# A tower of attention and experts on one core: waits per half and per expert, the last two pairs' expert copies on ScalarE alone, new slots for the last stage

## The reference, cut to what is computed

```python
B, S, C = 16, 512, 64            # 16 sequences of 512 tokens, 64 channels
x  = fourier_concat(ids)         # 24 features of a token
h  = LN(relu(x @ W1 + b1) @ W2 + b2) * gamma + beta + 0.1 * (x @ Wres + bres)
h  = h + attn(layernorm(h))      # 8 heads, scores 512x512, softmax, @ v, out weights Wo
f  = layernorm(h)
w  = top-2 softmax of (relu(f @ router_w1 + b) @ router_w2 + b)   # of 6 experts
y_e = relu(relu(f @ e1 + b1) @ e2 + b2) @ e3 + b3                 # every expert e
out = h + sum over the two chosen experts of w_e * y_e
```

## Time and profile before

| | us |
|---|---|
| median of 3 runs | 707.37 |
| lowest and highest | 705.65, 707.96 |
| the profiled execution, its own time | 705.38 |
| its span, first to last instruction | 703.6 |
| TensorE busy in the span | 650.5 |
| VectorE busy | 546.5 |
| ScalarE busy | 470.0 |
| GpSimd busy | 277.9 |

### The profile page before, as it was taken

One profiled execution on the slowest core, in us unless ns is written; L12 is line 12 of the kernel. 1 busy time (PEld: TensorE's weight loads), 2 busy tenths in 40 slices (PEclk: granted clock), 3 DMA queues, 4 the chain that ended last, 5 costly groups with the idle time before them and its releaser, 6 DMA issues.

```text
span 703.6 us, 26738 instructions
## 1 busy us (share of the span) xinstructions
PE 650.5 (92%) x11632; PEld 370.6 (53%) x11632; DVE 546.5 (78%) x1078; ACT 470.0 (67%) x1183; POOL 277.9 (39%) x354
## 2 busy tenths in 40 slices
PE   5789999999999999999999999999999999999974
PEld 4445555445645465545654465454664446554652
DVE  5687878787797877878787887978878788687657
ACT  2678885975668665886658766687558866678321
POOL 1242215315652175502853146620764119211173
PEclk9899999999999999999999999999999999999999
DMA  4000000000000000000000000000000000000001
GB/s 164 1 3 3 1 3 3 3 2 2 18 2 2 2 3 18 2 2 2 17 5 2 2 3 18 2 2 2 3 18 2 2 2 3 18 2 3 3 2 32
DMA packets 9428, 6.66 MB, mean 9 GB/s; under 512 B 8672, under 2 KB 8800, under 8 KB 9184
## 3 DMA queue, kind: packets, MB, share of 16 engines
q1 hardware_dynamic: 9312, 4.97, 2.4%
HBM read 2.87 MB, written 2.10 MB: 7 GB/s over the span
## 4 chain that ended last, share of the span: by engine, by line
PE 60%; DVE 22%; ACT 7%; issue 6%; POOL 4%; DMA 0%; SPq 0%; DVEq 0%; ACTq 0%; POOLq 0%
PE s_bank L525 23%; PE s_bank L494 17%; DVE nmax L899 8%; ACT p L786 5%; PE s_bank L609 5%; DVE e2t L1111 3%; PE s_bank L684 3%; PE s_bank L673 2%; PE s_bank L506 2%; DVE st L916 2%; PE s_bank L708 1%; DVE hatt L1095 1%; PE s_bank L588 1%; PE s_bank L535 1%; ACT e1t L834 1%
## 5 line engine op out<-in xcount | busy, mean ns | idle before, releaser
L786 ACT ACTIVATE p<-s_bank,nmax 128x512 f32<-128x512 f32 x512 | 347.8, 691 | 146.9 <-DVE nmax L899 145.8
L899 DVE TENSOR_REDUCE nmax<-s_bank 128x1 f32<-128x512 f32 x512 | 325.5, 681 | 50.2 <-PE s_bank L494 49.6
L494 PE MATMUL s_bank<-kf,g 64*64 64x512 f32 x2048 | 260.9, 594 | 6.4 <-DVE y L1126 2.8
L525 PE MATMUL s_bank<-p,woz 64*64 64x256 f32 x4096 | 247.1, 377 | 10.0 <-POOL woz L349 4.4
L525 PEld LDWEIGHTS s_bank<-p,woz 64*64 64x64 f32 x4096 | 163.6, 133 | 124.8 <-issue 45.9
L349 POOL TENSOR_TENSOR woz<-cst,rz 128x256 f32<-128x256 f32 x126 | 74.6, 613 | 264.0 <-DVE rz L905 264.0
L494 PEld LDWEIGHTS s_bank<-kf,g 64*64 64x64 f32 x2048 | 74.2, 133 | 91.3 <-issue 48.1
L786 ACT ACTIVATION_READ_ACCUMULATOR p<-s_bank,nmax 128x1 f32 x512 | 105.3, 206 | 0.0
L911 DVE STREAM_TRANSPOSE m<-s_bank 128x512 f32<-128x512 f32 x64 | 45.6, 712 | 26.1 <-PE s_bank L525 26.1
L1204 POOL TENSOR_TENSOR st<-st,power 128x8 f32<-128x8 f32 x24 | 39.5, 1648 | 45.3 <-DVE st L926 45.3
L358 POOL TENSOR_TENSOR y<-y,gt 128x768 f32<-128x768 f32 x28 | 41.3, 1475 | 37.9 <-DVE gt L1079 20.7
(11 more groups left out here) (117 smaller groups left out, 501.6 us busy)
## 6 DMA issues: line engine op xcount, KB each, us to landing
tower_out<-o SPq DMA_DIRECT2D x16, 128.0 KB, 2.7
cst<-consts SPq DMA_DIRECT2D x1, 1070.0 KB, 8.1
e2t<-ids SPq DMA_DIRECT2D x1, 896.0 KB, 5.4
cst<-consts SPq DMA_DIRECT2D x1, 416.0 KB, 5.9
cst<-consts SPq DMA_DIRECT2D x1, 288.0 KB, 3.6
e2t<-ids SPq DMA_DIRECT2D x1, 128.0 KB, 2.9
cst<-consts SPq DMA_DIRECT2D x1, 3.0 KB, 1.7
```

What stands on the lines that cost most here:

```text
L494: last = pe.matmul(double[half(q), 512 * r:512 * r + 512], g[half(r), a // 2 % 2, a % 2, first:first + 64], kf[half(r), par, a // 4, :], s ...
L525: last = pe.matmul(bank("PV", i, a)[half(q), 512 * hh:512 * hh + 256], woz[half(r), kept, 2 * mm + hh, :], keys[:, q, :, :], start=(part = ...
L786: nc.scalar.activation(p[:, 8 * kept + c % 8, :], bank("S", i, c - r)[:, 512 * r:512 * r + 512], ACT.Exp, bias=nmax[:, c % 16:c % 16 + 1], ...
L899: nc.vector.tensor_reduce(nmax[:, c % 16:c % 16 + 1], bank("S", i, c - r)[:, 512 * r:512 * r + 512], AX.X, ALU.max, negate=True).then_inc( ...
```

## The change

- `pv` waits for the first half of `woz` before `mm` 0 and for the second before `mm` 2, in all 64 products.
- Group 0 of the outputs waits for the copies of each of the three expert pairs before the two tiles of it, in all pairs.
- In pairs 6 and 7 ScalarE makes both tiles of each expert copy; VectorE makes none, and `e2_first` is gone.
- The bias products of pair 7 get slots of their own (`YB`); that of group 0 now stands before the last transposes.
- `Z` and `L` get new slots; from these `ring_places` gives other tiles from slot 22 of pair 7 on.

```diff
 Z = {'FIN': 11,
- 'LN2': 16,
- 'T': 22,
- 'T_ACT': 20,
- 'R': 23,
+ 'LN2': 17,
+ 'T': 23,
+ 'T_ACT': 22,
+ 'R': 24,
  'R_ACT': 23,
  'L': 24,
- 'GATE': (26, 26, 29, 31, 36, 42, 43),
- 'GATE_ACT': (25, 36),
- 'E1': (44, 47, 54),
- 'E1_ACT': (45, 47, 54),
- 'E2': (59, 62, 63),
- 'E2_DVE': (58, 64, 66),
- 'Y': (65, 72, 75, 77),
- 'Y_DVE': (69, 71, 74, 77)}
+ 'GATE': (25, 27, 27, 28, 36, 45, 69),
+ 'GATE_ACT': (25, 41),
+ 'E1': (40, 47, 49),
+ 'E1_ACT': (41, 47, 52),
+ 'E2': (55, 56, 63),
+ 'Y': (65, 73, 78, 82),
+ 'Y_DVE': (70, 71, 74, 76),
+ 'E2_ACT': (55, 61, 64)}
...
 L = {'FIN0': 63,
- 'FIN1': 0,
+ 'FIN1': 11,
...
- 'T': 12,
- 'T_ACT': 9,
- 'R': 13,
- 'R_ACT': 9,
- 'L': 28,
+ 'T': 20,
+ 'T_ACT': 0,
+ 'R': 31,
+ 'R_ACT': 2,
+ 'L': 38,
...
- 'E1': (23, 42, 45),
- 'E1_ACT': (15, 19, 24),
- 'E2': (43, 50, 55),
- 'E2_ACT': (28, 39, 53),
- 'E2_DVE': (35, 35, 35),
- 'Y': (57, 60, 62, 63),
- 'Y_DVE': (61, 62, 63, 63)}
+ 'E1': (21, 38, 40),
+ 'E1_ACT': (11, 19, 19),
+ 'E2': (38, 47, 51),
+ 'E2_ACT': (18, 37, 58),
+ 'YB': (19, 57, 63, 63),
+ 'Y': (57, 60, 63, 63),
+ 'Y_DVE': (61, 63, 63, 63)}
...
                 if part == 0:
                     free("PV", i, a)
-                    pe.wait_ge(wozd, 2 * (HH * i + a) + 2)
...
                 for mm in range(4):
+                    if not part and mm % 2 == 0:
+                        pe.wait_ge(wozd, 2 * (HH * i + a) + mm // 2 + 1)
                     for r in range(2):
...
                     if slot == f["Y"][j]:
-                        if j == 0:
-                            pe.wait_ge(e2_sb, EP * i + EP)
-                            if f is L:
-                                pe.wait_ge(e2_first, EP)
+                        if f is not L:
+                            free("Y", i, j)
                         for x in range(NE):
+                            if j == 0 and x % 2 == 0:
+                                pe.wait_ge(e2_sb, EP * i + x // 2 + 1)
...
-                    if f is L and slot == f["E2_ACT"][e]:
+                    if f is not F and slot == f["E2_ACT"][e]:
                         act.wait_ge(e2_ps, EP * i + e + 1)
-                        nc.scalar.activation(e2t[:, 2 * e, :], bank("E2", i, e)[:, 0:512], ACT.Relu,
-                                             bias=k("e2b")[:, 2 * e:2 * e + 1]).then_inc(e2_first, 1)
+                        for r in range(2):
+                            last = nc.scalar.activation(e2t[:, 2 * e + r, :], bank("E2", i, e)[:, 512 * r:512 * r + 512],
+                                                        ACT.Relu, bias=k("e2b")[:, 2 * e + r:2 * e + r + 1])
+                        last.then_inc(e2_sb, 1)
...
-                    if slot == f["E2_DVE"][e]:
+                    if f is F and slot == f["E2_DVE"][e]:
```

More of the change, by code:

```diff
@@ L116 @@
  'LN2': 8,
[L117 to L130 removed]
+ 'T': 20,
[3 more added lines that the diff above has]
+ 'L': 38,
+ 'GATE': (17, 20, 21, 24, 28, 34, 52),
+ 'GATE_ACT': (11, 57),
+ 'E1': (21, 38, 40),
[5 more added lines that the diff above has]
+ 'Y_DVE': (61, 63, 63, 63)}
 def at(slot, offset, i):
@@ L164, in ffn @@
         for j in range(4):
-            if slot == f["Y"][j]:
+            if slot == f["YB" if f is L else "Y"][j]:
                 order.append(("Y", i, j))
@@ L221, in read_at @@
     if name in ("E1", "E2", "Y"):
-        reader = "E1_ACT" if name == "E1" else "Y_DVE" if name == "Y" else "E2_DVE"
+        reader = "E1_ACT" if name == "E1" else "Y_DVE" if name == "Y" else "E2_DVE" if f is F else "E2_ACT"
         slot = f[reader][e]
@@ L320, in tower @@
             sem(x) for x in ("tok_half", "fin_ps", "fin_parts", "hatt_sb", "x2t_ps", "xt_sb", "rh_ps", "rh_sb", "l_ps", "gate", "gate_act")]
-        (e1_ps, e1_sb, e2_ps, e2_sb, e2_first, y_ps, y_sb, y_pool, y_dve, gated) = [
-            sem(x) for x in ("e1_ps", "e1_sb", "e2_ps", "e2_sb", "e2_first", "y_ps", "y_sb", "y_pool", "y_dve", "gated")]
+        (e1_ps, e1_sb, e2_ps, e2_sb, y_ps, y_sb, y_pool, y_dve, gated) = [
+            sem(x) for x in ("e1_ps", "e1_sb", "e2_ps", "e2_sb", "y_ps", "y_sb", "y_pool", "y_dve", "gated")]
         LN_DVE, LN_STEP = 4, (4, 3, 3)
@@ L690, in ffn_out @@
                 for j in range(4):
-                    if slot == f["Y"][j]:
-                        free("Y", i, j)
-                        double = bank("Y", i, j)
-                        if f is L:
-                            for c in range(2):
-                                for q in range(2):
-                                    pe.matmul(double[half(q), 512 * c:512 * c + NE * C], k("lead")[half(c), :],
-                                              k("e3b")[half(c), :], start=True, stop=False, skip_group_check=True)
-                        if j == 0:
-                            pe.wait_ge(e2_sb, EP * i + EP)
-                            if f is L:
-                                pe.wait_ge(e2_first, EP)
+                    double = bank("Y", i, j)
+                    if f is L and slot == f["YB"][j]:
+                        free("Y", i, j)
+                        for c in range(2):
+                            for q in range(2):
+                                pe.matmul(double[half(q), 512 * c:512 * c + NE * C], k("lead")[half(c), :],
+                                          k("e3b")[half(c), :], start=True, stop=False, skip_group_check=True)
+                    if slot == f["Y"][j]:
+                        if f is not L:
+                            free("Y", i, j)
                         for x in range(NE):
+                            if j == 0 and x % 2 == 0:
+                                pe.wait_ge(e2_sb, EP * i + x // 2 + 1)
                             for c in range(2):
@@ L1106, in ffn @@
                 for e in range(EP):
-                    if slot == f["E2_DVE"][e]:
+                    if f is F and slot == f["E2_DVE"][e]:
                         dve.wait_ge(e2_ps, EP * i + e + 1)
-                        for r in ((1,) if f is L else (0, 1)):
+                        for r in range(2):
                             last = nc.vector.tensor_scalar(
```

4 lines of the change are left out of this document (removed).

## The result

The changed kernel takes 703.27 us (median of 12 runs, 702.35 to 706.84), the kernel before in the same comparison 707.03 (12 runs, 704.82 to 708.05). The ratio is 0.9953, 95% interval 0.9942 to 0.9964: 3.3 us faster, with the bounds at 2.5 and 4.1. Four executions of the kernel before among all those of this document, of 722 to 1722 us, are left out of every figure.

What follows compares the result with a forecast made beforehand. TensorE, busy 92% of the span, was taken as the bound, so its waits decide. Terms -0.5 - 0.75 + 0.5 = -0.75 us from 706.5 gave 705.8 us; range 702.6 to 708.0, forecast itself 704.3 to 707.2.

Steps and rivals of the forecast that it cites:

- Pair 0, -0.5: Output weights' finer wait in pair 0: 0.61 us won, about 0.1 lost at the third product, so -0.5 us.
- Pairs 1 to 6, 0 for both waits: Finer waits for output weights and expert copies: time won is lost at the next waits, so 0.
- Last pair, -0.75: Stretch from 598 to 659 us: TensorE's new order, VectorE's moved gating part and other banks together give -0.75 us.
- +0.15, -0.70 and -0.20: Last pair: +0.15 to about 617.5 us, -0.70 from 626 to 635 us, -0.20 for other banks at 659.10.
- The third rival, ScalarE as the bound: Last pair: ScalarE's copies among the exponentials end too late, making the kernel slower, 708.2 or 709.2 us; chance 0.12.
- Last stage, +0.5: From 659 us to the end: between -0.35 at full clock and +0.8 if the clock falls; +0.5 taken.
- The product order up to the layer norm gives nothing: Start of the last stage: a moved part only fills TensorE while VectorE transposes; the norm starts as before.
- TensorE stands about as long before this point as it did: Last stage, where the clock fell: idle time 2.5 against 2.3 us, so +0.5, nearer the fallen case, was taken.
- Expert 1 lasts 0.86 us, so the gating and all that follows start 0.8 us later: Last stage after `xt`: expert 1 ahead of the router delays logits and gating by 0.8 us at the same clock.
- second rival: Clock stays at its upper level in the last stage: 704.9 us, or 703.7; chance 0.13.
- the sum at the full clock, -0.35: Last stage if the clock does not fall: second output at 693.05 instead of 693.38, so -0.35 us.
- the rival of waits that pay in every pair: Finer waits pay in each of six pairs: 702.9 us, or 699.9 if the weights' part stays too; chance 0.15.

Runs made afterwards that it cites:

- w_woz: Kernel before with one edit: the weighted sums wait for each half of the output weights; 706.15 us, ratio 0.9985.
- a_re: Changed kernel with the router's first product ahead of expert 1's first product in the last stage; 703.31 us, ratio 0.9953.
- a_half: Changed kernel with the second half of the last expert's copy in the last stage moved to VectorE; 703.03 us, ratio 0.9952.
- z_dve: Changed kernel with pair 6's expert copies made by VectorE instead of ScalarE, same slots; 703.35 us, ratio 0.9955.
- t_coarse: Changed kernel with both finer waits taken back, new slots and ScalarE's copies kept; 704.24 us, ratio 0.9953.
- a_less: Changed kernel with 4 filler products instead of 12 ahead of the last transposes of x2; 705.43 us, ratio 0.9974.
- b_fill: Kernel before with 20 filler products instead of 12 ahead of the last transposes of x2; 707.09 us, ratio 1.0000.
- ol_fill: Kernel before with both finer waits, new `Z` with its ScalarE copies, old last stage, and 20 filler products instead of 12; 707.03 us, ratio 1.0004.
- l_split: Changed kernel with the second half of each expert's copy in the last stage on VectorE; 706.81 us, ratio 1.0009.
- b_free: Kernel before with 20 filler products and pair 6's last two weighted sums cut to one channel of 64 (computes less); 703.36 us, ratio 0.9957.

## Why the prediction was right or wrong

**Pair 0, -0.5: right.** 0.57 us in w_woz; TensorE's wait fell from 1.42 to 0.85.

**Pairs 1 to 6, 0 for both waits: right.** 0.14 and 0.21 us over all six pairs. The rows named as "late next" took the time up: the exponential at 124 us (0.83 us, where the prediction said about 1.0), and for the outputs that of 179 us, with a bank wait at 173.46 that the prediction did not name. The pairs stay 82.55 us apart. The added satisfied waits cost nothing that a column shows.

**Last pair, -0.75: right in kind, a quarter too large, and that close only because errors of its terms cancel.** Its three terms were +0.15, -0.70 and -0.20. To the scores behind the router it gave +0.33 (617.35 before, 617.30 after, with 0.38 carried in). From there to the last expert product it gave -1.02 (658.07 before, 657.00 after): the 0.95 that the prediction took off went, and the 0.25 that it gave back for new waits did not come. The banks gave +0.13, not -0.20: by `ring_places` the two banks of this product now come from two blocks of scores, so the program waits for exponentials and no longer for the transpose, and TensorE stands 0.33 us there, 0.16 of it for an exponential by its row at 658.19. (The profile still puts 1.01 us of the weight load's idle time down to the transpose, which ends 0.1 us before the exponential does.) The third rival, ScalarE as the bound, did not come.

**Last stage, +0.5: the step that failed.** It gave -0.79 up to `x` and -0.36 behind it, -1.15 in all, so this term is off by 1.65 us and has the wrong sign. Three sentences of it were wrong.

"The product order up to the layer norm gives nothing": it gave 0.79 us in the profiles. Over all kernels, the seven with the old last table have 18.9 to 19.6 us in this column and the seven with the new one 17.8 to 18.6. The old timeline shows a hole in the first part of the last product, where TensorE waited for nothing that the profile names:

```profile
664.56 1.04 PE L525 MATMUL s_bank<-p,woz 64*64 64x256 f32 x15
666.23 3.31 PE L525 MATMUL s_bank<-p,woz 64*64 64x256 f32 x49 [0.64 <-issue]
```

These 64 steps took 4.98 us, in the changed kernel 3.97 (the row at 662.67 above), which has holes of 0.20 and 0.31 us further on instead. The same hole stands behind the same 15 steps in all seven kernels with the old table, 0.51 to 1.19 us long, and in none with the new one; taken off the fourth column it leaves 18.4 to 18.6 us in all seven, so it makes their scatter. What causes it was not tested.

"TensorE stands about as long before this point as it did": it stood 0.78 us, not 2.5. The third and fourth outputs of pair 6, the bias product and the filler now fill it up to 676.6 us. The prediction had noted the moved bias product in its second rival, and not added up its length (0.82 us at 688.67 in the trace before) with those around it. This is why the clock stayed up: in the profiles of the changed kernel, a_re, a_half and z_dve no wait of TensorE from the transposes of x2 on is over 0.90 us (in t_coarse one, of 1.55), and in all five the clock is 1.00 up to its last product. a_less puts the wait back, and with it the fall and 2.2 us.

"Expert 1 lasts 0.86 us, so the gating and all that follows start 0.8 us later": the first half is right (the logits stand 5.36 us behind `x`, and 4.42 in b_fill, which has the old order at the full clock); the second is not. The gating's last rank step stands 10.5 us behind `x` in before, after and b_fill alike. It goes by GpSimd's weighted sums for pair 6, which hold VectorE's two-operand steps, and these go by `x`. The rows for it were in the trace before: 0.80 and 0.49 us for steps that take 0.2 elsewhere in the same list, and the prediction took all of the gating's length as its own. VectorE's timeline of the kernel before, and GpSimd's beside it:

```profile
685.75 0.80 DVE L1043 TENSOR_TENSOR gt<-gt,gs 128x48 f32<-128x48 f32 x1
686.59 0.49 DVE L1045 TENSOR_TENSOR gt<-gt,cst 128x48 f32<-128x48 f32 x1
...
688.55 0.21 DVE L1060 TENSOR_TENSOR gt<-gt,cst 128x48 f32<-128x48 f32 x1
688.79 0.20 DVE L1062 TENSOR_REDUCE gs<-gt 128x8 f32<-128x48 f32 x1
...
685.49 0.99 POOL L366 TENSOR_TENSOR ys<-y 128x384 f32<-128x384 f32 x1
686.57 0.45 POOL L368 TENSOR_TENSOR ys<-ys 128x128 f32<-128x128 f32 x1
```

and VectorE's of the changed kernel, 10.49 us behind its `x`:

```profile
687.08 0.20 DVE L1063 TENSOR_REDUCE gs<-gt 128x8 f32<-128x48 f32 x1
```

The fall of the clock in the profile before therefore cost nothing up to there; it was hidden. Only what lies behind the gating pays. There the sum at the full clock, -0.35, was met in size (21.22 to 20.86 us from `x` to the last row) and not in its reason: without the finer wait for the copies the new order has 21.31 (t_coarse), so the slots and ScalarE's copies gave nothing here and the finer wait 0.45.

**From the profiles to the medians.** Columns 1 to 5 give 2.3 us, with the means of column 4 2.4, against 3.3 by the ratio. The runs without a profile have a time and a mean clock. Over three comparisons the kernel before had 15 runs at 0.991 with a median of 705.55 us (its profiled run is one like these, 705.38), 27 at 0.989 and 0.990 with 706.73, and 27 at 0.988 with 707.67. Of the changed kernel's twelve, eleven are between 702.35 and 704.17 at 0.989 to 0.994, and one at 0.982 took 706.84. So the old kernel's typical run loses 1 to 2 us more at the lower clock than its profiled one, and the changed kernel's seldom does. That these falls stand in the last stage, at places where nothing hides them (as in b_fill behind 691 us, 1.4 us), is likely from the four profiles that show such falls (b_fill, ol_fill, a_less, l_split). It isn't shown, since a fall in the head moves the start of the scores as well: it stands between 26.11 and 27.72 us in these profiles.

Of the rivals, "the clock stays at its upper level" is what happened, at 703.3 where it said 704.9 or 703.7 (its terms give 703.8 from 705.38); its evidence, the products moved ahead of the filler, was in hand and got 0.13. That 703.3 lies inside the range is luck: the lower end, 702.6, comes from the rival of waits that pay in every pair, which the runs refute, while the forecast itself reached down to 704.3 only.

## What to carry to other kernels

A finer wait pays only where nothing else is late within the period: of 14 shortened waits here the first and the last paid, 0.57 and 0.45 us. Before costing a delay at the end of a program, look at whether the steps behind it have the length that they have alone; if they are stretched by a neighbouring engine, an earlier input gives nothing (b_fill: inputs 1.2 us sooner, no gain) and less work on the neighbour gives the time back (b_free: 2.4 us at the gating's rank step, 3.7 with the clock). Add up TensorE's idle time in the new order before each place where the old trace shows a low granted clock; whether it is 0.8 or 2.4 us was worth more here than every removed wait.

## What was not expected of the hardware

- A VectorE operation on two SBUF operands of 128x48 took 1.53 us beside a GpSimd multiplication of 128x768, 0.80 beside a sum of 128x384, 0.21 with GpSimd at rest; reduces and operations on PSUM kept their 0.2 us beside the same work.
- The fall of the granted clock from 1.00 to 0.50 moved with the filler: with 8 more filler products it left 680 us and came at 692 us, behind the next wait (2.87 us). One program, with waits of 2.45 us, had runs at a mean clock from 0.984 to 0.992, 4.2 us apart. In ol_fill a wait of 1.54 us was followed by a fall, in t_coarse one of 1.55 us was not.
- TensorE stood 0.64 us in the middle of a product, with no wait in the program there, and took 1.0 us longer for its 64 steps than the changed kernel. The hole (0.51 to 1.19 us) is at the same step in all seven kernels with the old table; in the seven with the new one, holes of 0.20 to 0.86 us stand at other places of the last stage.
